# Value products of two attentions as three rounded products, with GpSimd splitting the values first in each unit

## The reference, cut to what matters

```python
x = x + tanh(g_xattn[0]) * L0_xattn(layernorm(x), ctx, ...)   # 16 heads of 96, 4 groups of keys and values
x = x + tanh(g_ffn[0])   * L0_ffn(layernorm(x), ...)
x = x + tanh(g_xattn[1]) * L1_xattn(layernorm(x), ctx, ...)   # 32 heads of 128, 8 groups, q and k rms-normed
x = x + tanh(g_ffn[1])   * L1_ffn(layernorm(x), ...)

# one attention
q = latents @ Wq.T;  k = hidden @ Wk.T;  v = hidden @ Wv.T
scores = einsum('bkgqd,bksd->bkgqs', q, k) * scale
attn   = softmax(scores)
out    = einsum('bkgqs,bksd->bkgqd', attn, v)                 # the value product: the change is here
return out @ Wo.T
```

## Time and profile before

| what | value |
|---|---|
| median of 3 runs | 2706.75 us (2701.5 to 2707.76) |
| the profiled execution | 2702.36 us, span 2700.5 us |
| attention of layer 0, first query product to last value product | about 850 to 1297 us |
| attention of layer 1, the same | about 1549 to 2483 us |
| busy: PE, DVE, ACT, POOL | 2461.5, 1362.8, 1016.6, 762.3 us |
| mean granted clock of PE | 0.949 of 2.4 GHz |

### The profile page before, as it was taken

One profiled execution on the slowest core, in us unless ns is written; L12 is line 12 of the kernel. 1 busy time (PEld: TensorE's weight loads), 2 busy tenths in 40 slices (PEclk: granted clock), 3 DMA queues, 4 the chain that ended last, 5 costly groups with the idle time before them and its releaser, 6 DMA issues. The chain is left out here.

```text
span 2700.5 us, 33590 instructions
## 1 busy us (share of the span) xinstructions
PE 2461.5 (91%) x12768; PEld 2170.6 (80%) x12768; DVE 1362.8 (50%) x2137; ACT 1016.6 (38%) x2306; POOL 762.3 (28%) x608
## 2 busy tenths in 40 slices
PE   8999999979998899999779689999999999999824
PEld 6888888778997688888579478999999999998713
DVE  6222222132202456666543446666666666666697
ACT  3222222132211555556300245445455455454323
POOL 3000000000003233342021065556555555552120
PEclk9999999989998799999989899999999999999667
DMA  6222222162233123222021123333323333322001
GB/s 202 71 71 71 70 70 61 40 211 78 92 94 97 49 85 90 81 78 72 12 70 40 38 78 96 98 95 104 98 93 104 100 93 100 103 83 78 6 0 49
DMA packets 159361, 217.46 MB, mean 81 GB/s; under 512 B 31510, under 2 KB 124082, under 8 KB 158178
## 3 DMA queue, kind: packets, MB, share of 16 engines
q1 hardware_dynamic: 159202, 215.33, 26.4%
HBM read 176.99 MB, written 38.29 MB: 80 GB/s over the span
## 5 line engine op out<-in xcount | busy, mean ns | idle before, releaser
L1060 POOL TENSOR_TENSOR attend_w_hi<-attend_w_raw,attend_one 128x1024 fp32r<-128x1024 f32 (+1 forms) x184 | 337.4, 1834 | 301.7 <-PE attend_ps_gemm L1352 201.8
L1216 DVE TENSOR_TENSOR attend_w_lo<-attend_w_raw,attend_w_hi 128x1024 fp32r<-128x1024 f32 (+1 forms) x184 | 250.5, 1363 | 174.4 <-POOL attend_w_hi L1060 173.8
L1352 PE MATMUL attend_ps_gemm<-normed_hi,attend_w_hi 128*128 128x400 f32 x704 | 267.0, 379 | 37.5 <-DVE attend_w_lo L1216 37.5
L1352 PE MATMUL attend_ps_gemm<-attend_o_hi,attend_w_hi 128*128 128x400 f32 x704 | 251.4, 357 | 7.1 <-issue 3.5
L1125 ACT ACTIVATE attend_p<-attend_p,attend_neg_max 100x361 f32<-100x361 f32 x256 | 150.7, 590 | 266.1 <-DVE attend_neg_max L1255 266.1
L1352 PE MATMUL attend_ps_gemm<-attend_o_hi,attend_w_lo 128*128 128x400 f32 x704 | 244.0, 347 | 0.0
L1352 PE MATMUL attend_ps_gemm<-attend_o_lo,attend_w_hi 128*128 128x400 f32 x704 | 243.8, 346 | 0.0
L1352 PE MATMUL attend_ps_gemm<-normed_lo,attend_w_hi 128*128 128x400 f32 x704 | 243.7, 346 | 0.0
L1352 PE MATMUL attend_ps_gemm<-normed_hi,attend_w_lo 128*128 128x400 f32 x704 | 242.9, 345 | 0.0
L1431 PE MATMUL attend_ps_out<-attend_pt,attend_v_in 121*128 121x400 f32 (+4 forms) x640 | 239.1, 512 | 1.7 <-DVE attend_pt L1273 1.7
L1134 ACT ACTIVATE attend_p<-attend_p,attend_exp_inv 100x361 f32<-100x361 f32 (+1 forms) x384 | 207.4, 616 | 0.0
(11 more groups left out here) (262 smaller groups left out, 5726.8 us busy)
## 6 DMA issues: line engine op xcount, KB each, us to landing
attend_w_raw<-in_wq SPq DMA_DIRECT2D x88, 512.0 KB, 4.2
attend_w_raw<-in_wo SPq DMA_DIRECT2D x64, 512.0 KB, 3.6
attend_w_raw<-in_wo SPq DMA_DIRECT2D x32, 384.0 KB, 3.5
context_ctx_raw<-in_ctxT SPq DMA_DIRECT2D x8, 1456.0 KB, 7.0
attend_k_raw<-scratch_k SPq DMA_DIRECT2D x64, 180.5 KB, 3.8
context_ctx_raw<-in_ctxF SPq DMA_DIRECT2D x22, 512.0 KB
scratch_v<-context_v_out SPq DMA_DIRECT2D x44, 256.0 KB, 2.2
scratch_k<-context_kt_out SPq DMA_DIRECT2D x44, 256.0 KB, 5.0
```

Source lines behind the costliest of these rows:

```text
L1060: pool.tensor_tensor(hi, w_flat(w_raw, j % RAW, j), one[:hi.shape[0]].to_broadcast(hi.shape), ALU.mult).then_inc(w_hi_done, 1)
L1216: dve.tensor_tensor(w_flat(w_lo, j % SPLIT, j), w_flat(w_raw, j % RAW, j), w_flat(w_hi, j % SPLIT, j).bitcast(F32), ALU.subtract).then_inc ...
L1352: mm = pe.matmul(out, left[a](c), right[b](c), start=(c == 0 and a == b == 0), stop=(c == chunks - 1 and a == 1))
```

## The change

The value product becomes three rounded products per chunk, as the others are. For that the values are split by POOL into v_hi and v_lo (one buffer each, first in the unit, after the value product of the unit before), ACT copies every chunk of the turned weights into pt_hi, and DVE makes every remainder pt_lo (one buffer each instead of two). A bank of ps_turn is free when DVE has made its remainder. The slots of values go from three to two, freed when POOL has split them, the raw weight slots of layer 0 from three to two, and one memset is added; SP's first load of values waits for it. What a unit issues on POOL and DVE changes in order as the diff shows.

```diff
-    RAW, SPLIT = 3 - layer, 3
-    P_SLOTS, K_SLOTS, V_SLOTS = 3, 2, 3
+    RAW, SPLIT = 2, 3
+    P_SLOTS, K_SLOTS, V_SLOTS = 3, 2, 2
...
-        pt = sb("pt", [KR, 2, NCH, HG * S])
+        v_hi = sb("v_hi", [KR, NCH, HD], F32R)
+        v_lo = sb("v_lo", [KR, NCH, HD], F32R)
+        pt_hi = sb("pt_hi", [KR, NCH, HG * S], F32R)
+        pt_lo = sb("pt_lo", [KR, NCH, HG * S], F32R)
...
SP, values(u):
                 if u >= V_SLOTS:
-                    sp.wait_ge(pv_done, u - V_SLOTS + 1)
+                    sp.wait_ge(v_lo_done, u - V_SLOTS + 1)
...
-            for u in range(V_SLOTS - 1):
+            sp.wait_ge(consts, CONSTS)
+            for u in range(V_SLOTS):
                 values(u)
...
                 keys(u + K_SLOTS + 1)
-                values(u + V_SLOTS - 1)
+                values(u + V_SLOTS)
...
POOL:
+            pool.memset(v_in[:, :, NCH - 1], 0.0).then_inc(consts, 1)
...
+            def split_values(u):
+                if u >= NU:
+                    return
+                slot = u % V_SLOTS
+                pool.wait_ge(v_load[slot], (u // V_SLOTS + 1) * 16 * V_DMAS)
+                if u:
+                    pool.wait_ge(pv_done, u)
+                pool.tensor_tensor(v_hi[:], v_in[:, slot], one[:KR].unsqueeze(2).to_broadcast([KR, NCH, HD]), ALU.mult
+                                   ).then_inc(v_hi_done, 1)
+                pool.wait_ge(v_hi_done, u + 1)
+                pool.tensor_tensor(v_lo[:], v_in[:, slot], v_hi[:].bitcast(F32), ALU.subtract
+                                   ).then_inc(v_lo_done, 1)
...
             for u in range(NU):
+                split_values(u)
                 for j in output_tiles(u + 1):
                     weights(j)
                 split_keys(u + 3)
...
ACT, copy_turn(u, kc):
-                if u >= 2:
-                    act.wait_ge(pv_done, u - 1)
-                act.activation(pt[:ROWS[kc], u % 2, kc], ps_turn[:ROWS[kc], 0, :HG * S], ACT.Copy
-                               ).then_inc(turn_read[0], 1)
+                if u:
+                    act.wait_ge(pv_done, u)
+                act.activation(pt_hi[:ROWS[kc], kc], ps_turn[:ROWS[kc], kc % 2, :HG * S], ACT.Copy).then_inc(turn_hi_done, 1)
...
                 copy_turn(u, 0)
+                copy_turn(u, 1)
                 exps(u + 2, 0)
                 copy_turn(u, 2)
+                if NCH == 4:
+                    copy_turn(u, 3)
                 normalise(u + 1)
...
DVE:
-            def copy_turn(u, kc):
-                dve.wait_ge(turned, u * NCH + kc + 1)
-                if u >= 2:
-                    dve.wait_ge(pv_done, u - 1)
-                dve.tensor_copy(pt[:ROWS[kc], u % 2, kc], ps_turn[:ROWS[kc], 1, :HG * S]).then_inc(turn_read[1], 1)
+            def remainder_turn(u, kc):
+                dve.wait_ge(turn_hi_done, u * NCH + kc + 1)
+                dve.tensor_tensor(pt_lo[:ROWS[kc], kc], ps_turn[:ROWS[kc], kc % 2, :HG * S], pt_hi[:ROWS[kc], kc].bitcast(F32),
+                                  ALU.subtract).then_inc(turn_lo_done, 1)
...
-                copy_turn(u, 1)
+                remainder_turn(u, 0)
+                remainder_turn(u, 1)
                 invert(u + 1)
                 maxima(u + 2, 0)
                 for j in output_tiles(u + 1)[:SPLIT]:
                     split(j)
                 if u >= HB:
                     accumulate(u - HB, 0)
+                remainder_turn(u, 2)
                 if NCH == 4:
-                    copy_turn(u, 3)
+                    remainder_turn(u, 3)
                 if u >= HB:
                     accumulate(u - HB, 1)
...
PE, turns(u, kc):
-                before = reads_before[t][kc % 2]
-                if before:
-                    pe.wait_ge(turn_read[kc % 2], before)
+                last = t - (2 if NCH == 4 else (1, 3, 2)[kc])
+                if last >= 0:
+                    pe.wait_ge(turn_lo_done, last + 1)
...
PE, weigh_values(u):
-                pe.wait_ge(v_load[u % V_SLOTS], (u // V_SLOTS + 1) * 16 * V_DMAS)
+                pe.wait_ge(v_lo_done, u + 1)
                 for kc in range(NCH):
-                    pe.wait_ge(turn_read[kc % 2], reads_before[u * NCH + kc + 1][kc % 2])
-                    mm = pe.matmul(ps_out[:HD, :HG * S], v_in[:ROWS[kc], u % V_SLOTS, kc], pt[:ROWS[kc], u % 2, kc],
-                                   start=(kc == 0), stop=(kc == NCH - 1))
+                    pe.wait_ge(turn_lo_done, u * NCH + kc + 1)
+                    rows = slice(0, ROWS[kc])
+                    for a, b in ((v_hi, pt_hi), (v_lo, pt_hi), (v_hi, pt_lo)):
+                        mm = pe.matmul(ps_out[:HD, :HG * S], a[rows, kc], b[rows, kc],
+                                       start=(kc == 0 and a is v_hi and b is pt_hi), stop=(kc == NCH - 1 and b is pt_lo))
```

More of the change, by code:

```diff
@@ L883, in attend @@
         k_load = [sem("k_load0"), sem("k_load1")]
-        v_load = [sem("v_load0"), sem("v_load1"), sem("v_load2")]
+        v_load = [sem("v_load0"), sem("v_load1")]
+        v_hi_done = sem("v_hi_done")
+        v_lo_done = sem("v_lo_done")
         k_hi_done = sem("k_hi_done")
@@ L897, in attend @@
         turned = sem("turned")
-        turn_read = [sem("turn_read_act"), sem("turn_read_dve")]
+        turn_hi_done = sem("turn_hi_done")
+        turn_lo_done = sem("turn_lo_done")
         pv_done = sem("pv_done")
@@ L945, in tokens_of @@
             return slice(s * HT, (s + 1) * HT)
-        reads_before = [[0, 0]]
-        for t in range(NU * NCH):
-            last = list(reads_before[-1])
-            last[t % NCH % 2] += 1
-            reads_before.append(last)
         def w_view(w, j):
@@ L970, in step_tiles @@
             return output_tiles(u) + query_tiles(u)
+        CONSTS = 12 if layer == 1 else 5
         @block.sync
@@ L1027, in _ @@
                 keys(u + K_SLOTS + 1)
-                values(u + V_SLOTS - 1)
+                values(u + V_SLOTS)
                 for j in step_tiles(u + 2):
                     tile(j)
-        CONSTS = 11 if layer == 1 else 4
         @block.gpsimd
```

## The result

The changed kernel takes 2732.65 us (median of 4 runs, 2730.67 to 2733.88), the kernel before 2706.91 beside it: a ratio of 1.0095, 95% interval 1.0082 to 1.0108, so 25.7 us slower. Its profiled execution took 2732.43 us with a span of 2730.6, 30.1 us more than the span before.

The account below looks back on a forecast made before the run. PE was taken to bound the kernel, busy 2461.5 of 2700.5 us. Layer 1 steady units +6.0, its ends +0.4 and layer 0 +1.3 made +7.7 on 2702.4: 2710, plus 4.4 to the median, said as 2715; range 2690 to 2735.

Parts of the forecast that it names:

- the forecast's own case: Whole kernel: slower, the forecast and beyond, 2715 to 2730 us; chance 0.31.
- PE's saving: Value product, three rounded products per chunk: 0.38 us less per layer 1 unit, 0.49 per layer 0 unit, 40 us unhindered.
- The steady stall: Layer 1, units 4 to 56: PE waits 0.38 us for chunk 2's remainder, cancelling the saving; +0.45 per block, +6.0 us.
- k = 2: Layer 1, one of a block's four units: DVE's query weight split runs beside POOL's squares; +0.33 us.
- The rival that the stall does not form: Layer 1 steady units: remainder 0.38 us earlier, all PE's saving stays, 2684 us; half gives 2700; together chance 0.24.
- POOL's price: POOL's two-instruction split of the values in each unit: 1.88 us, upper bound 2.76.
- The ends of layer 1: Layer 1, units 0 to 3 and 57 to 63: together +0.4 us.
- Unit 3: Layer 1, no output products: value product starts early and stalls 2.65 us for chunk 2's remainder; less 0.38, +2.3 us.
- Units 57 to 63: -1.5: Layer 1's end: DVE's round, about 10.0 us, passes PE's 9.3, with 2 us in hand at first; -1.5 us.
- the five stalled ones: Layer 0, units 5, 9, 13, 17, 21: PE's chunk 2 turn waits for chunk 0's remainder; +0.8 each, +4.0 us.
- Units 25 to 29: Layer 0: the round from one exponential to the next becomes 10.7 us against 10.11; +0.6 each, +3.0 us.
- "What costs nothing": Fewer raw weight slots in layer 0, later values loads, the memset and single turned-weight buffers: no cost.

Follow-up runs that it names:

- run 1: Changed kernel with POOL making the next unit's output weight before splitting the values, both layers, all units but the last: 2707.6 us, 1.0009 of the kernel before.
- run 2: Changed kernel with DVE making the remainder of chunk 2 ahead of the output weight's split, in layer 1 alone: 2712.4 us, 1.0029 of the kernel before.
- run 3: Changed kernel with the order edits of run 1 and run 2 together: 2714.9 us, 1.0035 of the kernel before.
- run 8: Changed kernel without POOL's remainder of the values; the second product repeats the first, so the output is off: 2710.4 us, 1.0017 of the kernel before.
- run 5: Changed kernel with the third raw weight slot of layer 0 given back: 2727.7 us, 1.0084 of the kernel before.
- run 4: Changed kernel with DVE's remainders of chunks 2 and 3 (layer 1: chunk 2) ahead of the output weight splits, last units only: 2729.9 us, 1.0088.
- run 6: Changed kernel with DVE splitting the third output weight behind the output's remainder, in each layer's last unit: 2721.7 us, 1.0059 of the kernel before.
- run 9: Changed kernel without DVE's remainders of the turned weights; the third product repeats the rounded weights, so the output is off: 2673.3 us, 0.9878.

## Why the prediction was right

2715 was forecast, slower, range 2690 to 2735; 2732.65 lies inside it near its upper end, just beyond the 2715 to 2730 that the forecast's own case named. The mechanism stands. The size does not: the sum was +7.7 and the spans differ by 30.1. That the range held is in part luck: it ends 2.4 us above the measured time, and 22 of the 30 us were not in the sum, most of them in the last units, between the layers and behind a wait in unit 3.

**PE's saving**: 0.38 and 0.49 a unit. Shown, by the 16 units of layer 0 (-0.48 to -0.52) and by runs 1, 2, 3 and 8 in layer 1 (-0.37 to -0.40).

**The steady stall**: predicted were the rounded weight at +6.54, the remainder done at +9.37, PE at +9.47; in unit 24 +6.53 (1.90 us from 1959.72), +9.38 and +9.44. The chain of nine terms held to 0.03; its one term without a row, 0.1 for the wake-up, measured 0.06. A block was +0.45 and is +0.72. More than half of the difference is k = 2: 0.44 to 0.51 for 0.33, which no run takes apart. The rest is 0.02 to 0.07 in each of the others; in unit 24 (+0.09) it is the first product after the wait, 0.28 to the next start instead of 0.18, which the chain did not have. The rival that the stall does not form decided at 0.38 us of lead. Runs 1, 2 and 8 are that rival, made true: their steady units gave 23.4 to 23.7 us against the changed kernel, but against the kernel before only 14, not the 20 of the prediction, since the units with k = 1 wait for the sums with or without the stall.

**POOL's price**: from the start of the values' split to the start of the output weight are 1.89 us in unit 24 (1.88 predicted); no `v_lo` in the changed kernel takes over 1.04 us, so none collides.

**The ends of layer 1**: the step that was mis-sized most, +0.4 for +16.8. Three things in it. (a) Unit 3: the stall of 2.65 is there (2.79), but the clock was not in the sum. The windows of unit 3 are the wait with what is around it, and the query product (length, PE, PEld, DVE, ACT, POOL busy, PEclk, DMA share, GB/s):

```profile
1648.50:1653.70 5.20, 2.42 (x9) 2.08 (x10) 3.41 (x5) 3.54 (x9) 5.12 (x4) 0.79 0.26 57
1653.70:1660.20 6.50, 6.50 (x25) 6.47 (x25) 2.49 (x3) 1.66 (x5) 1.01 (x1) 0.65 0.35 110
```

PE is granted 0.65 on average over the query product, some of it at 1.2 GHz and the rest at 2.4, and the product takes 6.5 us instead of 4.4. The same wait and the query product behind it in run 5:

```profile
1649.18 0.45 PE L1452 MATMUL attend_ps_out<-attend_pt_hi,attend_v_hi 119*128 119x400 f32 x1 [2.80 <-DVE attend_pt_lo L1289]
...
1649.80:1654.20 4.40, 4.40 (x26) 4.40 (x25) 2.64 (x4) 1.66 (x5) 1.53 (x1) 1.00 0.30 111
```

There the clock stays at 2.4 GHz, the product takes 4.4 us, and unit 3 costs +2.8, near the predicted +2.3. Runs 4 and 6, with waits of 2.78 and 2.79, lie between (+4.3 both). So the wait is the change's price and holds, while the drop behind it, 2.6 us here, differs between kernels that agree up to that point; what decides it stays open. In run 2, without the wait, unit 3 costs +0.97. (b) Units 57 to 62: I let DVE's round have 2 us in hand; it had not, and units 58, 59 and 60 pay +1.23, +0.41 and +1.63 (run 9, without DVE's remainders, has +0.4 for the three together). The loss of unit 58 goes with POOL's order alone (-0.36 in run 1), that of unit 60 does not (+1.62). (c) The last unit. "Units 57 to 63: -1.5" has no term for the third output weight, though the prediction names this very queue for layer 0 ("DVE's remainders stand behind the last weight splits"). Runs 4 and 6 show it: without that split ahead, 6.3 us come back.

**Layer 0**: 16 units and the five stalled ones as predicted (-8.0 and +3.4). Run 9 shows that the latter are waits for remainders. Units 25 to 29 were over-priced. The last units were +2.1 and are +5.8.

**"What costs nothing"** was wrong in one point: the third raw slot. It does cost nothing where layer 1's steady units were taken as the witness; in the last unit, where three weights are wanted in one unit, it costs 3.5 us (run 5). The rest of that paragraph held: PE never waits for `v_lo`, nor POOL for a load of the values.

**Left open**: the +3.1 us between the layers. The first query product of layer 1 is 4.7 us later after the change, and in run 6, where the last unit of layer 0 is mended, 0.8 us earlier than before, so most of it hangs on how layer 0 ends; by which of the transfers was not tried.

A row of the prediction needs a correction of its place: the earlier trace rows stands at the end of unit 57, ahead of unit 58.

## What to carry to other kernels

Price a change at the instruction that it makes late on each queue, and then look at everything that stands behind that instruction: here 1.88 us on an engine that was 28% busy came out as a wait on the one that was 91% busy, through a third. Do this separately for the steady units, the units in which one kind of work is missing, and the last unit: the same order of two instructions gained 0.38 us a unit in one stretch and lost up to 4.3 us a unit in another, and a buffer slot that was free in 31 units of layer 0 cost 3.5 us in the last. When a wait is moved rather than removed (run 4), the instruction to move is the one that itself waits (run 6). And before a gain is credited to a change, give the kernel before the same repairs.

## What the runs showed of the hardware

The collision between POOL and DVE, which the prediction bounded at 0.88 us and did not expect for the values, comes as soon as the order puts them beside the weight split. POOL and DVE in unit 25 of run 1:

```profile
1967.51 1.89 POOL L1088 TENSOR_TENSOR attend_v_lo<-attend_v_in,attend_v_hi 121x384 fp32r<-121x384 f32 x1
1969.36 0.79 POOL L1072 TENSOR_TENSOR attend_k_hi<-attend_k_raw,attend_one 128x362 fp32r<-128x362 f32 x1
1970.23 0.96 POOL L1075 TENSOR_TENSOR attend_k_lo<-attend_k_raw,attend_k_hi 128x362 fp32r<-128x362 f32 x1
...
1966.68 1.83 DVE L1237 TENSOR_TENSOR attend_w_lo<-attend_w_raw,attend_w_hi 128x1024 fp32r<-128x1024 f32 x1
```

`v_lo` takes 1.89 us instead of 1.03 and the remainder of the keys 0.96 instead of 1.84: the price stays the same and goes to whichever of POOL's two subtractions lies beside DVE's. Of 96 of each, 55 of `v_lo` and 5 of the keys take over 1.5 us in run 1, none and 60 in the changed kernel. The Trainium skill ("GPSIMD Engine Reference", section 8) has GpSimd contend with DVE instructions of two SBUF inputs; the trace agrees, 0.86 us here.

The second is the clock. One wait of 2.79 us on PE was followed by 6.5 us at a mean granted clock of 0.65, and unit 3 cost 2.6 us more than in run 5, where a wait of 2.80 us was followed by a clock of 1.00. So a wait of this length can bring the drop and need not. Waits of 0.6 us, twice a block, were followed by none (1.00 over units 4 to 56).
